# Gated messages of a graph network: gate operands in PSUM, five blocks a bank, rows added in seven operations, edge features loaded three batches ahead

## The chip, the core and the metric

The kernel runs on one core of a Trainium2 chip. Its engines are PE (TensorE, matmuls), DVE (VectorE), ACT (ScalarE), POOL (GpSimd, which here issues the indirect gathers) and SP (SyncE, which issues the plain transfers). The metric is the time of the whole program on the device, in microseconds (us), as the median of several runs. Lower is better.

## The reference, cut to what matters

Four graph layers follow one another on 6,250 nodes with 96 features and 200,000 edges sorted by destination. The change touches only the edge part of the third, the layer of gated messages:

```python
edge_input = concatenate([x[src], edge_attr], axis=-1)        # 96 + 32 features
messages = gelu(edge_input @ mW1 + mb1) @ mW2 + mb2
gates = sigmoid(gelu(edge_input @ gW1 + gb1) @ gW2 + gb2)     # one number per edge
aggregated = segment_sum(messages * gates, dst, num_segments=N)
```

## The kernel before, in words

The node parts `x @ mW1` and `x @ gW1` are computed once per node and stored in DRAM as `table_mg`, a row of 2 x 96 numbers per node (message half, gate half). The edges are padded and cut into 128 contiguous chunks, one per partition; a step takes one edge of every chunk, and `U` = 14 steps make a batch. There are `BATCHES` = 112 batches, 1,568 steps. The fast path of the stage is the function `sum_pass` of each engine; a batch n goes as follows.

- **SP** (L619 to L634) loads the batch's edge features, transposed, 256 KB, into one of two slots of `EA`, and waits until PE is done with the slot (`edge_product`, L622). In its loop, in order: the load for batch k+2, the wait for the running sums of batch k, the store of these sums to `run_m` (L633).
- **PE** (L1193 to L1200) multiplies them with block-diagonal weights `BD`: four edges stand in a group of 128 partitions, each edge giving 2 x 96 columns. A matmul gives two edges, 384 columns, in a bank of PSUM; `BANKS` = 7 products a batch. Eight banks `p_h` are used in turn, so PE runs ahead of ACT by eight products.
- **ACT** copies each product to `hid` in SBUF (`keep_edges`, L1574 to L1582), two batches ahead (`AHEAD_E`); there are four slots. For batch n it applies gelu to two halves (L1591), then tanh to the 14 logits per partition (L1593, `gates`; a sigmoid is written as half of 1 + tanh of the half), then copies the products of batch n+2.
- **POOL** (L824 to L828) issues 14 gathers per batch, one per step: 128 rows of `table_mg`, chosen by a column of indices `sources` in SBUF, into one of two slots of `rows`. The instruction stands at L790. Gathers of batch k wait for the additions of batch k-2 (`rows_added`, L826).
- **DVE** (L2229 to L2269) adds the gathered rows to `hid` in two operations of 1,344 elements per partition (L2235). It then makes the running sums of batch n-1, 14 dependent operations of 97 elements (L2263), and the messages of batch n: the gate half times the gate weights (L2243), the sum over features (L2246), then, after ACT's tanh, message half times (gate + 1) (L2248) and the gate's own column (L2250). The loop is `add_rows(n)`, `run_sums(n - 1)`, `messages(n)`.

So the order on each engine is written out by hand, and counts of semaphores couple them: `edge_product`, `edges_kept`, `rows_landed`, `rows_added`, `gelu_done`, `logit_ready`, `gate_ready`, `sums_ready`, `sums_stored`. The gate weights `gate_row` are a row repeated on all partitions in SBUF (`gw2`), and `gates` a part of the SBUF tile `small`. Before the stage, node matmuls (L1098, with DVE's L2136 emptying their banks) run beside the first two batches' gathers; behind it, the sums at each node's last edge are gathered from `run_m` (also L790) and the node part of the layer follows.

Of the kernel before, what the change touches and what calls it, by code (L numbers as in the profile page):

```python
# [11 lines left out]
ALU = mybir.AluOpType  # L12
ACT = mybir.ActivationFunctionType
# [4 lines left out]
D = 96  # L18
# [11 lines left out]
CH = P  # L30
U = 14
# [3 lines left out]
BATCHES = 2 * ITER  # L35
# [3 lines left out]
EG = 4  # L39
UG = -(-U // EG)  # L40
PIECES = 4
BANKS = 7
assert U == 2 * BANKS
ROOM = 16
AHEAD_E = 2
SLOTS_E = 4
MW = D + 1
AW = D + HEADS
ACCS = 3
# [88 lines left out]
def build(nc, x, src, dst, row_heads, src_rows, dst_rows, edge_t, consts, weights, bias, gcn_b, scalars, gate_w, mg_edge, qk_w, out):  # L138
# [21 lines left out]
    with ExitStack() as ctx:  # L160
# [24 lines left out]
        EA = sb("EA", [P, 2, UG, CH])  # L185
# [11 lines left out]
        small = sb("small", [CH, 4, U * HEADS])  # L197
# [5 lines left out]
        gw2 = sb("gw2", [P, D])  # L203
        sc = sb("sc", [P, 2])
        BD = sb("BD", [P, EG, 2, D])
# [132 lines left out]
        p_tr = [ps(f"p_tr{k}", [P, 512]) for k in (0, 1)]  # L338
        p_mm = [ps(f"p_mm{k}", [P, 512]) for k in (0, 1)]
        p_c = [*p_tr, *p_mm]  # L340
        p_four = ps("p_e", [P, 4, 512])
        p_e = [p_four[:, k, :] for k in range(4)]
        p_h = [*p_e, *p_tr, *p_mm]
        p_pair = p_four[:, 0:2, :]
        p_last = [p_e[HEADS - 1], p_tr[1]]
        p_sums = p_tr[0]
        gate_row = gw2[0:CH, :]
        gates = small[:, 1, 0:U]
        rows = GA[0:CH, 0:2 * U * 2 * D].rearrange("p (h u f) -> p h u f", h=2, u=U)
        hid_at = [*[GA[0:CH, (2 + k) * U * 2 * D:(3 + k) * U * 2 * D] for k in range(SLOTS_E - 1)], VA[0:CH, 0:U * 2 * D]]  # L350
        hid = [a.rearrange("p (u f) -> p u f", u=U) for a in hid_at]
# [116 lines left out]
        def wait(eng, s, v):  # L468

            if not isinstance(v, int) or v > 0:  # L470
                eng.wait_ge(s, v)
# [51 lines left out]
        def products(groups, n_w):  # L523

            return sum(len(bank_tiles(g, n_w)) for g in range(groups))

        def acc_steps(a):

            return len(range(a, U, ACCS))
# [38 lines left out]
        def _(sp):  # L568
# [49 lines left out]
            def sum_pass():  # L618

                def load_batch(k):  # L620
                    if k >= 2:
                        sp.wait_ge(edge_product, BANKS * (k - 1))  # L622
                    sp.dma_start(EA[:, k % 2, :, :], edge_t[:, UG * k:UG * (k + 1), :]).then_inc(edge_landed[k % 2], 16)
                load_batch(0)
                load_batch(1)
                sp.wait_ge(rows_cleared, 1)
                sp.dma_start(run_m[E:E + 2 * P, :].rearrange("(p k) f -> p k f", k=2), R[:, 1, 0:2, :]
                             ).then_inc(spares_stored, 16)
                for k in range(BATCHES):
                    if k + 2 < BATCHES:  # L630
                        load_batch(k + 2)
                    sp.wait_ge(sums_ready[k % 2], k // 2 + 1)
                    sp.dma_start(by_chunk(run_m[0:E, :])[:, U * k:U * (k + 1), :], R[:, k % 2, :, :]  # L633
                                 ).then_inc(sums_stored[k % 2], 16)  # L634
# [153 lines left out]
        def _(pool):  # L788
# [31 lines left out]
            def sum_pass():  # L820

                pool.wait_ge(sources_landed, 16)
                pool.wait_ge(table_stored, 16 * GROUPS * 2)
                for k in range(2 * ITER):  # L824

                    wait(pool, rows_added, 2 * (k - 1))  # L826
                    for j in range(U):
                        gather(rows[:, k % 2, j, :], table_mg, sources[:, U * k + j:U * k + j + 1], rows_landed[k % 2])  # L828

                pool.wait_ge(sums_ready[1], ITER)  # L830
                pool.indirect_dma_start(out=run_m, out_offset=bass.IndirectOffsetOnAxis(ap=open_at[:, 0:1], axis=0),
                                        in_=R[:, 1, U - 1, :], in_offset=None, compute_op=ALU.add).then_inc(open_added, 16)
                pool.wait_ge(nodes_landed, 32)
                for h in (0, 1):
                    pool.wait_ge(sums_stored[h], 16 * ITER)
                pool.wait_ge(open_added, 16)
                for t in range(TILES):
                    gather(AGG[:, t, :], run_m, ends[:, t:t + 1], ends_landed[t // GRP])
# [80 lines left out]
        def _(pe):  # L919
# [267 lines left out]
            def sum_pass():  # L1187


                pe.wait_ge(hT_ready, at["turn"])  # L1190
                pe.wait_ge(product_used, at["mm"])

                for m in range(BANKS * BATCHES):  # L1193
                    n, k = m // BANKS, m % BANKS
                    if k == 0:
                        pe.wait_ge(edge_landed[n % 2], 16 * (n // 2 + 1))
                    wait(pe, edges_kept, m - len(p_h) + 1)
                    pe.matmul(p_h[m % len(p_h)][0:CH, 0:4 * D], EA[:, n % 2, k // 2, :],  # L1198
                              BD[:, 2 * (k % 2):2 * (k % 2) + 2, :, :].rearrange("p a b f -> p (a b f)"),
                              start=True, stop=True).then_inc(edge_product, 1)  # L1200
                pe.wait_ge(edges_kept, BANKS * BATCHES)
                update_nodes()

            def scatter_pass(n):
# [176 lines left out]
        def _(act):  # L1381
# [190 lines left out]
            def sum_pass():  # L1572

                def keep_edges(n):  # L1574

                    wait(act, sums_ready[n % 2], (n - SLOTS_E) // 2 + 1)
                    for k in range(BANKS):
                        m = BANKS * n + k
                        act.wait_ge(edge_product, m + 1)
                        act.activation(hid[n % SLOTS_E][:, 2 * k:2 * k + 2, :],  # L1580
                                       p_h[m % len(p_h)][0:CH, 0:4 * D].rearrange("p (a f) -> p a f", a=2), ACT.Copy
                                       ).then_inc(edges_kept, 1)  # L1582

                act.wait_ge(table_stored, 16 * GROUPS * 2)
                for n in range(AHEAD_E):
                    keep_edges(n)
                for n in range(BATCHES):
                    for c in (0, 1):
                        half = hid[n % SLOTS_E][:, BANKS * c:BANKS * (c + 1), :]
                        act.wait_ge(rows_added, 2 * n + c + 1)  # L1590
                        act.activation(half, half, ACT.Gelu).then_inc(gelu_done, 1)  # L1591
                    act.wait_ge(logit_ready, n + 1)
                    act.activation(gates, small[:, 0, 0:U], ACT.Tanh, bias=half_bias, scale=0.5).then_inc(gate_ready, 1)  # L1593
                    if n + AHEAD_E < BATCHES:
                        keep_edges(n + AHEAD_E)
# [117 lines left out]
        def _(dve):  # L1713
# [510 lines left out]
            def sum_pass():  # L2224

                dve.tensor_scalar(half_bias, sc[0:CH, 1:2], 0.5, None, ALU.mult)
                dve.drain()

                def add_rows(n):  # L2229

                    dve.wait_ge(edges_kept, BANKS * (n + 1))
                    dve.wait_ge(rows_landed[n % 2], 16 * U * (n // 2 + 1))
                    for c in (0, 1):
                        half = hid[n % SLOTS_E][:, BANKS * c:BANKS * (c + 1), :]
                        dve.tensor_tensor(half, half, rows[:, n % 2, BANKS * c:BANKS * (c + 1), :], ALU.add  # L2235
                                          ).then_inc(rows_added, 1)

                def messages(n):

# [357 lines left out]
```

## Time and profile before

| what | value |
|---|---|
| median of 3 runs | 5472.3 us (5466.99 to 5479.78) |
| profiled execution, its own time | 5465.93 us |
| its span, first to last instruction | 5464.0 us |
| busy in the span: PE, DVE, ACT, POOL | 3652, 3789, 2527, 3537 us |
| gathers of `table_mg`, start of the first and of the last | 1519.8 and 3842.4 us of the span |

The page of the profile gives for each group of instructions its source line, engine, operation, tiles and shapes, the count behind an x, the busy time and mean duration, and the idle time of that engine just before with what ended it. "issue" is time in which an engine waited for nothing that the profile shows. SPq is the queue in which SP issues transfers. Times in a timeline are microseconds from the start of the span. POOL's rows are rougher than those of the other engines.

### The profile page before, as it was taken

What the parts mean: (1) busy time and instruction counts of PE and PEld (TensorE: products, weight loads), DVE (VectorE), ACT (ScalarE), POOL (GpSimd) and SP (SyncE); (2) the same over time, 40 slices, a digit from 0 to 9 for tenths busy, and PEclk for the clock granted to TensorE, in tenths of its full rate; (3) what the DMA queues carried; (4) which work ended last, traced back from release to release, by engine and by line L of the source; (5) the groups of instructions that cost most, each with busy time, mean ns of one, the idle gap of its engine ahead of it and who ended that gap; (6) DMA issues with size and microseconds to landing.
All of it is one profiled execution on the core that took longest, in us unless ns stands there. A gap on an engine that the chain in (4) does not pass through costs nothing.

```text
span 5464.0 us, 92238 instructions
## 1 busy us (share of the span) xinstructions
PE 3652.2 (67%) x33772; PEld 2286.6 (42%) x33772; DVE 3789.0 (69%) x5678; ACT 2527.0 (46%) x4379; POOL 3536.7 (65%) x2920
## 2 busy tenths in 40 slices
PE   4899899999953333333333333333279999999999
PEld 3888899899931111111111111111233333333333
DVE  7999432544455665665665655655379999999999
ACT  5999110101023233233333233332158888888887
POOL 3699100000057777777777777777448888888888
PEclk9999999999966666666666666666589999999999
DMA  3344889698733333333333333333111212222121
GB/s 70 165 200 191 331 340 394 256 398 336 292 90 115 117 114 115 118 110 117 117 110 119 117 111 117 117 111 118 46 35 57 64 57 60 60 58 64 57 63 38
DMA packets 296561, 760.10 MB, mean 139 GB/s; under 512 B 81161, under 2 KB 183753, under 8 KB 289993
## 3 DMA queue, kind: packets, MB, share of 16 engines
q1 hardware_dynamic: 217496, 595.47, 29.4%
q0 software_dynamic: 78768, 160.85, 11.2%
q8 instruction: 167, 2.74, 0.2%
q14 instruction: 130, 1.06, 0.1%
HBM read 589.77 MB, written 166.38 MB: 138 GB/s over the span
## 4 chain that ended last, share of the span: by engine, by line
PE 41%; POOL 34%; issue 15%; DVE 6%; ACT 1%; another core or an unknown queue 1%; DVEq 1%; DMA 0%; ACTq 0%; POOLq 0%; SPq 0%
POOL GA L790 32%; PE p_e L1167 14%; PE p_tr L1307 10%; PE p_e L1292 9%; PE p_mm L1269 3%; PE p_mm L1098 1%; POOL VA L790 1%; DVE VA L2423 1%; PE p_tr L1026 1%; DVE VA L1965 1%; POOL VA L902 1%; PE p_tr L1085 1%; DVE VA L1963 1%; PE p_e L1244 0%
## 5 line engine op out<-in xcount | busy, mean ns | idle before, releaser
L790 POOL DMA_INDIRECT GA<-table_mg,VA x1568 | 1791.1, 1142 | 1487.9 <-DMA table_mg<-VA 955.4
L2423 DVE TENSOR_TENSOR VA<-VA,p_mm 128x1024 f32<-128x1024 f32 (+1 forms) x1204 | 1362.0, 1203 | 7.5 <-POOL VA L902 6.6
L902 POOL TENSOR_SCALAR VA<-VA 128x1024 f32<-128x1024 f32 (+1 forms) x1204 | 1236.2, 1046 | 168.8 <-ACT VA L1644 157.0
L1198 PE MATMUL p_e<-BD,EA 128*128 128x384 f32 x784 | 407.1, 671 | 731.9 <-DMA EA<-in_edge_t 731.3
L1644 ACT ACTIVATE VA<-p_e 128x1024 f32<-128x1024 f32 x602 | 615.8, 1023 | 178.6 <-PE p_e L1292 177.5
L1307 PE MATMUL p_tr<-VA,GA 128*32 128x512 f32 (+1 forms) x5096 | 641.8, 580 | 2.7 <-ACT GA L1664 2.1
L2235 DVE TENSOR_TENSOR GA<-GA 128x1344 f32<-128x1344 f32 x168 | 254.2, 1554 | 542.7 <-DMA GA<-table_mg,VA 530.1
L2263 DVE SCALAR_TENSOR_TENSOR R<-R,keep,M 128x97 f32<-128x97 f32 x1568 | 505.8, 323 | 124.8 <-issue 8.2
L1198 PEld LDWEIGHTS p_e<-BD,EA 128*128 128x128 f32 x784 | 205.0, 270 | 916.9 <-DMA EA<-in_edge_t 765.1
L1198 PE MATMUL p_tr<-BD,EA 128*128 128x384 f32 x392 | 210.8, 669 | 370.9 <-DMA EA<-in_edge_t 370.9
L1198 PE MATMUL p_mm<-BD,EA 128*128 128x384 f32 x392 | 207.4, 660 | 374.0 <-DMA EA<-in_edge_t 374.0
L1292 PE MATMUL p_e<-T,GA 32*128 32x512 f16 x4632 | 444.9, 380 | 1.8 <-DVE GA L2392 1.1
L815 POOL TENSOR_TENSOR T<-T,B 128x192 f32 (+1 forms) x23 | 383.8, 16719 | 72.1 <-DVE T L1938 72.1
L1593 ACT ACTIVATE small<-small 128x14 f32<-128x14 f32 x112 | 34.4, 307 | 844.4 <-DVE small L2246 844.4
L1167 PE MATMUL p_e<-GA 128*128 128x192 f16 x4802 | 412.2, 246 | 0.0
L1167 PE MATMUL p_e<-GA,VA 128*128 128x192 f16 x4802 | 412.2, 246 | 0.0
L1167 PEld LDWEIGHTS p_e<-GA,VA 128*128 128x128 f16 x4802 | 397.7, 98 | 0.0
L1167 PEld LDWEIGHTS p_e<-GA 128*128 128x128 f16 x4802 | 397.6, 98 | 0.3 <-DVE M L2179 0.3
L1512 ACT ACTIVATE hT<-p_tr 96x512 f32<-96x512 f32 (+1 forms) x91 | 51.1, 567 | 717.3 <-PE p_tr L1085 689.3
L1646 ACT ACTIVATE VA<-p_e 128x512 f32<-128x512 f32 x602 | 356.3, 592 | 0.0
L2176 DVE SCALAR_TENSOR_TENSOR M<-p_e,dinv_s,T 128x96 f32<-128x96 f32 x196 | 62.3, 318 | 399.3 <-PE p_e L1167 399.1
L1198 PEld LDWEIGHTS p_tr<-BD,EA 128*128 128x128 f32 x392 | 102.8, 271 | 464.2 <-DMA EA<-in_edge_t 388.1
(267 smaller groups left out, 6616.6 us busy)
## 6 DMA issues: line engine op xcount, KB each, us to landing
GA<-adj SPq DMA_DIRECT2D x98, 800.0 KB, 6.1
VA<-adj SPq DMA_DIRECT2D x98, 800.0 KB, 6.1
run_m<-R SPq DMA_DIRECT2D x112, 700.0 KB, 3.9
GA<-adj SPq DMA_DIRECT2D x98, 768.0 KB, 6.1
VA<-adj SPq DMA_DIRECT2D x98, 768.0 KB, 6.1
H<-adj SPq DMA_DIRECT2D x56, 896.0 KB, 5.1
adj<-GA SPq DMA_DIRECT2D x25, 1568.0 KB, 5.3
adj<-VA SPq DMA_DIRECT2D x24, 1568.0 KB, 5.3
```

What stands on the lines that cost most here:

```text
L790: pool.indirect_dma_start(out=to, out_offset=None, in_=of, in_offset=bass.IndirectOffsetOnAxis(ap=at, axis=0)).then_inc(s, 16)
L815: pool.tensor_tensor(pair, pair, bias_row, ALU.add).then_inc(biased, 2)
L902: pool.tensor_scalar(e, e, HIGH, LOW, ALU.min, ALU.max).then_inc(clipped, 1)
L1167: mm = pe.matmul(p_e[b % 2][:, 0:PARTS * D], blk[b][:, s * P:(s + 1) * P], parts[:, s, :, :].rearrange("p k f -> p (k f)"), start=s == 0, ...
L1198: pe.matmul(p_h[m % len(p_h)][0:CH, 0:4 * D], EA[:, n % 2, k // 2, :], BD[:, 2 * (k % 2):2 * (k % 2) + 2, :, :].rearrange("p a b f -> p (a ...
L1292: mm = pe.matmul(to(e, cols), kT[rows, k // 2, d * P:(d + 1) * P], qT[b][rows, k % 2, 0:across(b)], start=k == 0, stop=k == 2, tile_positi ...
L1307: mm = pe.matmul(p_sums[e * HW:(e + 1) * HW, 0:across(b)], Vt[:, d, e, :], slot[n % SLOTS][:, e, i * across(b):(i + 1) * across(b)], start ...
L1644: act.activation(e[:, 0:2, :], p_pair[:, :, 0:cols], ACT.Exp, scale=HEADS_UNIT ** -2).then_inc(exps_ready, 1)
L1646: act.activation(e[:, 2, :], p_e[2][:, 0:cols], ACT.Exp, scale=HEADS_UNIT ** -2).then_inc(exps_ready, 1)
L2235: dve.tensor_tensor(half, half, rows[:, n % 2, BANKS * c:BANKS * (c + 1), :], ALU.add).then_inc(rows_added, 1)
L2263: op = dve.scalar_tensor_tensor(out=R[:, h, j, 0:MW], in0=before, scalar=keep[:, step:step + 1], in1=M[:, j, 0:MW], op0=ALU.mult, op1=ALU.add)
L2423: dve.tensor_tensor(e, e, p_mm[n % 2][:, 0:cols_of(n)].unsqueeze(1).to_broadcast([P, 2, cols_of(n)]), ALU.mult).then_inc(weighed, 1)
```

## The change

Constants: products are packed by `PACK` = 5 blocks of 96 columns, so a batch's 28 blocks take `PACKS` = 6 banks (480 columns, the last 288). `ADDS` = 7 additions a batch. PE's packs cross the groups of four edges, so a pack is one or two matmuls: nine products of one to five blocks for a batch. PSUM's last bank is taken out of the rotation (seven are left) and holds the gate weights, copied there once, and the gates. ACT's gelu is cut 8 steps and 6 steps. SP loads three batches before the loop and keeps that lead; there are still two slots of `EA`.

```diff
+PACK = 5
+PACKS = -(-2 * U // PACK)
+ADDS = BANKS
@@ build
-        p_h = [*p_e, *p_tr, *p_mm]
+        p_h = [*p_e, *p_tr, p_mm[0]]
-        gate_row = gw2[0:CH, :]
-        gates = small[:, 1, 0:U]
+        gate_row = p_mm[1][0:CH, 0:D]
+        gates = p_mm[1][0:CH, D:D + U]
+        def pack_halves(b):
+            return range(PACK * b, min(PACK * b + PACK, 2 * U))
+        def pack_cols(b):
+            return slice(D * pack_halves(b).start, D * pack_halves(b).stop)
@@ SP
-                        sp.wait_ge(edge_product, BANKS * (k - 1))
+                        sp.wait_ge(edge_product, PACKS * (k - 1))
-                load_batch(0)
-                load_batch(1)
+                for k in range(AHEAD_E + 1):
+                    load_batch(k)
...
-                    if k + 2 < BATCHES:
-                        load_batch(k + 2)
+                    if k + AHEAD_E + 1 < BATCHES:
+                        load_batch(k + AHEAD_E + 1)
@@ POOL
-                    wait(pool, rows_added, 2 * (k - 1))
+                    wait(pool, rows_added, ADDS * (k - 1))
@@ PE
-                for m in range(BANKS * BATCHES):
-                    n, k = m // BANKS, m % BANKS
-                    if k == 0:
+                for m in range(PACKS * BATCHES):
+                    n, b = m // PACKS, m % PACKS
+                    if b == 0:
                         pe.wait_ge(edge_landed[n % 2], 16 * (n // 2 + 1))
                     wait(pe, edges_kept, m - len(p_h) + 1)
-                    pe.matmul(p_h[m % len(p_h)][0:CH, 0:4 * D], EA[:, n % 2, k // 2, :],
-                              BD[:, 2 * (k % 2):2 * (k % 2) + 2, :, :].rearrange("p a b f -> p (a b f)"),
-                              start=True, stop=True).then_inc(edge_product, 1)
+                    at_col = 0
+                    for g in range(UG):
+                        part = [v for v in pack_halves(b) if v // (2 * EG) == g]
+                        if not part:
+                            continue
+                        cols = slice(D * (part[0] - 2 * EG * g), D * (part[-1] + 1 - 2 * EG * g))
+                        mm = pe.matmul(p_h[m % len(p_h)][0:CH, at_col:at_col + D * len(part)], EA[:, n % 2, g, :],
+                                       BD[:, :, :, :].rearrange("p a b f -> p (a b f)")[:, cols], start=True, stop=True)
+                        at_col += D * len(part)
+                    mm.then_inc(edge_product, 1)
@@ ACT
-                    for k in range(BANKS):
-                        m = BANKS * n + k
+                    for b in range(PACKS):
+                        m = PACKS * n + b
                         act.wait_ge(edge_product, m + 1)
-                        act.activation(hid[n % SLOTS_E][:, 2 * k:2 * k + 2, :],
-                                       p_h[m % len(p_h)][0:CH, 0:4 * D].rearrange("p (a f) -> p a f", a=2), ACT.Copy
-                                       ).then_inc(edges_kept, 1)
+                        act.activation(hid_at[n % SLOTS_E][:, pack_cols(b)], p_h[m % len(p_h)][0:CH, 0:D * len(pack_halves(b))],
+                                       ACT.Copy).then_inc(edges_kept, 1)
...
-                    for c in (0, 1):
-                        half = hid[n % SLOTS_E][:, BANKS * c:BANKS * (c + 1), :]
-                        act.wait_ge(rows_added, 2 * n + c + 1)
-                        act.activation(half, half, ACT.Gelu).then_inc(gelu_done, 1)
+                    for lo, hi in ((0, BANKS // 2 + 1), (BANKS // 2 + 1, BANKS)):
+                        some = hid[n % SLOTS_E][:, 2 * lo:2 * hi, :]
+                        act.wait_ge(rows_added, BANKS * n + hi)
+                        act.activation(some, some, ACT.Gelu).then_inc(gelu_done, 1)
@@ DVE
                 dve.tensor_scalar(half_bias, sc[0:CH, 1:2], 0.5, None, ALU.mult)
+                dve.tensor_copy(gate_row, gw2[0:CH, :])
                 dve.drain()
...
-                    dve.wait_ge(edges_kept, BANKS * (n + 1))
+                    dve.wait_ge(edges_kept, PACKS * (n + 1))
                     dve.wait_ge(rows_landed[n % 2], 16 * U * (n // 2 + 1))
-                    for c in (0, 1):
-                        half = hid[n % SLOTS_E][:, BANKS * c:BANKS * (c + 1), :]
-                        dve.tensor_tensor(half, half, rows[:, n % 2, BANKS * c:BANKS * (c + 1), :], ALU.add
-                                          ).then_inc(rows_added, 1)
+                    for k in range(BANKS):
+                        two = hid[n % SLOTS_E][:, 2 * k:2 * k + 2, :]
+                        dve.tensor_tensor(two, two, rows[:, n % 2, 2 * k:2 * k + 2, :], ALU.add).then_inc(rows_added, 1)
```

## Rows read from the trace of the kernel before

**Rows 1.** Busy time per engine from 1600 to 3800 us, inside the stage

```profile
core 0: us, PE busy (x) PEld busy (x) DVE busy (x) ACT busy (x) POOL busy (x), PEclk, DMA share, GB/s
1600.00:3800.00 2200.00, 752.02 (x1502) 394.79 (x1503) 1320.64 (x2144) 684.07 (x1072) 1717.77 (x1500) 0.67 0.38 115
```

**Rows 2.** Chain of waits from 1600 to 3800 us, by line

```profile
by line: POOL GA L790 78.1%; issue 21.9%
```

**Rows 3.** POOL's groups from 1600 to 3800 us: count, busy, mean ns, idle before

```profile
L790 POOL DMA_INDIRECT GA<-table_mg,VA x1500 | 1718.1, 1145 | 482.5 <-issue 482.5
```

**Rows 4.** Timeline of POOL, gathers 1, 28 and 29: start, duration, idle before

```profile
1519.82 0.97 POOL L790 DMA_INDIRECT GA<-table_mg,VA  x1 [955.42 <-DMA table_mg<-VA]
...
1553.67 0.95 POOL L790 DMA_INDIRECT GA<-table_mg,VA  x1 [0.30 <-issue]
1584.47 0.95 POOL L790 DMA_INDIRECT GA<-table_mg,VA  x1 [29.84 <-DVE GA L2235]
```

**Rows 5.** Timeline of one batch, DVE's operations and the gathers over them

```profile
2510.05 3.02 DVE L2235 TENSOR_TENSOR GA<-GA 128x1344 f32<-128x1344 f32 x2 [6.24 <-DMA GA<-table_mg,VA]
2511.11 1.33 POOL L790 DMA_INDIRECT GA<-table_mg,VA  x1 [0.30 <-issue]
...
2512.74 1.16 POOL L790 DMA_INDIRECT GA<-table_mg,VA  x1 [0.30 <-issue]
2513.17 5.48 DVE L2263 SCALAR_TENSOR_TENSOR R<-R,keep,M 128x97 f32<-128x97 f32 x14
...
2518.74 1.56 DVE L2243 TENSOR_TENSOR M<-GA,gw 128x1344 f32<-128x1344 f32 x1
...
2519.21 1.90 POOL L790 DMA_INDIRECT GA<-table_mg,VA  x1 [0.30 <-issue]
2520.37 1.55 DVE L2246 TENSOR_REDUCE small<-M 128x14 f32<-128x1344 f32 x1
2521.42 0.94 POOL L790 DMA_INDIRECT GA<-table_mg,VA  x1 [0.30 <-issue]
...
2522.30 1.56 DVE L2248 SCALAR_TENSOR_TENSOR M<-small,GA 128x1344 f32<-128x1344 f32 x1 [0.37 <-ACT small L1593]
2522.67 2.01 POOL L790 DMA_INDIRECT GA<-table_mg,VA  x1 [0.30 <-issue]
```

**Rows 6.** Timeline: a batch's last gather, the next adds, a late gather

```profile
2527.49 0.95 POOL L790 DMA_INDIRECT GA<-table_mg,VA  x1 [0.30 <-issue]
...
2530.22 3.03 DVE L2235 TENSOR_TENSOR VA<-VA,GA 128x1344 f32<-128x1344 f32 x2 [6.28 <-DMA GA<-table_mg,VA]
...
2531.94 2.13 POOL L790 DMA_INDIRECT GA<-table_mg,VA  x1 [2.25 <-issue]
```

**Rows 7.** Attention, later: POOL's L902 and DVE's L2423, ns min/median/max, first and last start

```profile
L902 POOL TENSOR_SCALAR VA<-VA x1204: 827/1042/1365, 4058.4 to 5453.0; 128x1024 f32<-128x1024 f32 x170, 128x768 f32<-128x768 f32 x2
...
L2423 DVE TENSOR_TENSOR VA<-VA,p_mm x1204: 894/1206/1222, 4059.6 to 5454.5; 128x1024 f32<-128x1024 f32 x170, 128x768 f32<-128x768 f32 x2
```

**Rows 8.** DVE lines over the whole span, ns min/median/max, first and last start

```profile
L2263 DVE SCALAR_TENSOR_TENSOR R<-R,keep,M x1568: 320/321/389, 1593.8 to 3864.3; 128x97 f32<-128x97 f32 x196
...
L2235 DVE TENSOR_TENSOR GA<-GA x168: 1548/1553/1560, 1581.2 to 3826.4; 128x1344 f32<-128x1344 f32 x168
...
L2136 DVE TENSOR_TENSOR T<-p_mm,B x38: 247/350/559, 1488.7 to 1570.4; 128x192 f32<-128x192 f32 x24, 128x384 f32<-128x384 f32 x12, 128x96 f32<-128x96 f32 x2
```

**Rows 9.** Timeline of one batch: edge load, tanh, PE's products, ACT's first and last copy

```profile
2519.05 0.43 SPq L623 DMA_DIRECT2D EA<-in_edge_t  x1
...
2521.96 0.31 ACT L1593 ACTIVATE small<-small 128x14 f32<-128x14 f32 x1 [7.52 <-DVE small L2246]
...
2523.24 4.67 PE L1198 MATMUL p_e<-BD,EA 128*128 128x384 f32 x8 [13.49 <-DMA EA<-in_edge_t]
...
2524.99 0.49 ACT L1580 ACTIVATE GA<-p_e 128x384 f32<-128x384 f32 x1 [2.72 <-PE p_e L1198]
...
2529.88 0.49 ACT L1580 ACTIVATE GA<-p_mm 128x384 f32<-128x384 f32 x1 [0.15 <-PE p_mm L1198]
```

More of the change, by code:

```diff
@@ L1191, in sum_pass @@
                 pe.wait_ge(product_used, at["mm"])
-                for m in range(BANKS * BATCHES):
-                    n, k = m // BANKS, m % BANKS
-                    if k == 0:
+                for m in range(PACKS * BATCHES):
+                    n, b = m // PACKS, m % PACKS
+                    if b == 0:
                         pe.wait_ge(edge_landed[n % 2], 16 * (n // 2 + 1))
                     wait(pe, edges_kept, m - len(p_h) + 1)
-                    pe.matmul(p_h[m % len(p_h)][0:CH, 0:4 * D], EA[:, n % 2, k // 2, :],
-                              BD[:, 2 * (k % 2):2 * (k % 2) + 2, :, :].rearrange("p a b f -> p (a b f)"),
-                              start=True, stop=True).then_inc(edge_product, 1)
-                pe.wait_ge(edges_kept, BANKS * BATCHES)
+                    at_col = 0
[8 more added lines that the diff above has]
+                    mm.then_inc(edge_product, 1)
+                pe.wait_ge(edges_kept, PACKS * BATCHES)
                 update_nodes()
```

## The prediction

> **What bounds the kernel now.** I read the stage first: the gated messages run from 1,520 to 3,865 us, and in the 2,200 us from 1,600 to 3,800 no engine is full: POOL is busy for 1,718 us, DVE for 1,321, PE for 752, ACT for 684, DMA for 0.38 of the time [rows 1]. So a busy share doesn't settle it. The chain of waits of the same stretch does: 78.1% POOL's gathers (L790), 21.9% "issue", which is the pause between one gather and the next, and nothing else [rows 2]. POOL is the bound, gather after gather, and its share is under 100% only because the 0.30 us pauses are not counted as busy.
>
> The pace: 1,500 gathers in 2,200 us are 1.467 us each [rows 3], and a batch of 14 takes 20.53 us. The same gathers alone, while DVE has hardly begun, start (1553.67 - 1519.82) / 27 = 1.254 us apart [rows 4]; a batch would take 17.55 us. So 2.98 us a batch are stalls of POOL, over 110 batches (of 1,568 gathers 28 are issued before the first add; 1,540 / 14 = 110) 328 us. That is all that there is to win here.
>
> Where the stalls lie: in one batch gathers of 0.94 to 0.95 us stand beside one of 1.90, which ends 0.81 us after the product with the gate weights (L2243), and one of 2.01, which ends 0.82 us after the gating (L2248). The gather begun during the reduction (L2246) takes 0.94, those of 1.33 and 1.16 end 0.84 and 0.82 us after the first and the second add (L2235), and those over the 14 running sums (L2263) show nothing [rows 5]. So a gather needs, about 0.13 us after its start, something that a long DVE operation with two SBUF operands holds, and gets it when that operation ends. Per batch: L2243 0.95, L2248 1.06, together 2.01; what is left of 2.98, 0.97, goes to the two adds: mostly 0.38 + 0.21 = 0.59, and in some batches more, where the next gather starts 1.95 us late and then takes 2.13 [rows 6].
>
> **The change, part by part.**
> (a) Gate weights and gates in PSUM. L2243 and L2248 keep one SBUF input each. No row shows a gather over such a long operation; the nearest is in the attention: POOL's L902, 1,024 elements read from and written to SBUF, has a median of 1,042 ns, beside DVE's L2423, which reads SBUF and PSUM, writes SBUF and is at work all the time [rows 7]. Were it held off as gathers are here, it couldn't keep that pace. The reduction, one SBUF input, stalls nothing either. Bounds: 0 to 2.01 us a batch gained; I take 2.01, the nearer rows. The two DVE operations cost what they did: 384 elements with one PSUM operand take 559 ns at most and 1,024 take 1,206 [rows 7, 8], so 1,344 come to 559 + 960 x 1.011 = 1,530 ns against 1,559. Unseen is the gates' repeated read of one PSUM word; from the nearest rows it costs nothing, and DVE has room for 3.7 us (below). The one copy of the weights is some 0.2 us in all.
> The Trainium skill, "SBUF — State Buffer", section "Who interferes with whom", says that a DVE instruction with two SBUF inputs contends with GpSimd reads and one with at most one doesn't, but infers that a tensor_tensor takes only the read side and leaves descriptor generation, which writes, alone. The trace disagrees with that inference: the 1.90 us gather. If writes are what matters, moving an input gains nothing: that is rival B, priced from rows.
>
> (b) Seven adds for two. Each 384 elements: the first 0.56 us, the next at 1.47 - 960 x 1.04 ns = 0.47 us intervals (1.47 us is what the second 1,344-element add puts on top of 1.55, and (1553 - 559) / 960 = 1.04 ns an element) [rows 5, 8]: 3.40 us against 3.03. A gather waits for the end of one such add, not of 1.5 us. The adds start 2.73 us after the last gather of their batch [rows 6]; undisturbed gathers ask at 2.64 and 3.89 us after it, the second 1.16 us into the adds, in the third of them, and waits 0.3; the next asks 1.25 us later, near the end of the sixth, and waits 0.1 to 0.2. So 0.4 us a batch against 0.97. Bounds: nothing, as over the running sums of 321 ns, which have pauses between them; and 2.2 us, if back to back adds let nobody in until the last ends (3.4 - 1.2). I take 0.4, because between the two adds of now a gather does get in: it ended 0.84 us after the first, in the middle of the second [rows 5]. Gain 0.57.
>
> (c) Five blocks a bank. ACT's copies (L1580) change from seven of 0.49 us to, scaled by their columns, five of 0.61 and one of 0.37 [rows 9], PE's matmuls from 14 (two for a product) to 18 for the same 2,688 columns; PE at 34% has room [rows 1]. Neither is on the chain. PE has seven banks instead of eight, more than one batch of six.
>
> (d) Edge features three ahead. Now the load for batch k+2 is issued at 2519.05, PE starts on it at 2523.24, ACT, idle since its tanh ended at 2522.27, gets a product at 2524.99 and ends its copies at 2530.37 [rows 9], 20.3 us after the adds began, as the next adds begin. With the load a batch earlier the products wait in their banks, and ACT is done 12.6 + 4.2 = 16.8 us after the adds begin (tanh's end now 12.2, the adds 0.4 longer; copies 3.4 and five pauses of 0.15); its gelu is due about 19.9 (a batch of 17.95 and four adds). This pays nothing now, since the 5.5 us of running sums between adds and L2243 hide ACT's delay, but it keeps ACT clear of the shorter batch. SP's wait for PE's batch k+1 stands ahead of the store of sums k: PE finishes that batch once ACT has copied batch k, over a batch before SP asks. At the start the third load stands ahead of the spare rows' store, which DVE wants only two batches on. I cost (c) and (d) at nothing.
>
> **Who is next.** DVE's chain in a batch, from the adds to the end of L2248, is 2523.86 - 2510.05 = 13.8 us [rows 5], then 14.2; POOL's batch becomes 17.55 + 0.4 = 17.95, so DVE still idles 3.7 us for the last row and POOL stays the bound. The rows' slots: gathers of batch n+2 need the adds of n, finished some 14 us before.
>
> **The sum.** 110 x (2.01 + 0.57) = 284 us gained; about 1 us lost at the two ends (three more tenths of adds before the first and after the last gather, the copy). The profiled execution took 5465.9 us, so 5183; it stands 6.4 us under the median of the three runs, 5472.3, for which I say 5189.
>
> **Rivals.**
> A, the forecast: chance 0.80.
> B, PSUM doesn't free POOL: what holds it is DVE's stream of 1,344 elements written to SBUF, which L2243 and L2248 keep. For it: all three stalling operations write 1,344, the reduction 14. Against it: L902 beside L2423, which writes as much. Gain 110 x 0.57 = 63: 5409. Chance 0.08.
> C, the seven adds hold as one: 2.2 us a batch stay: 110 x (2.98 - 2.2) = 86 gained: 5386. For it the back to back adds, against it the gather let in between two. Chance 0.07.
> D, slower: the writes hold POOL as in B, and the adds are one unbroken stream of them. Then 2.01 stays and 2.2 replaces 0.97: 110 x 1.23 = 135 us more: 5607. It decides from the point where the adds cost over 0.97 us a batch with the other two unchanged. Against it both rows above at once. Chance 0.03.
> E, DVE becomes the bound because the broadcast read of PSUM is slow. From L2248 at 1.56 + 3.7 = 5.3 us on it takes gain away, from 7.8 us on (3.9 ns an element more than any row shows) the kernel is slower. Chance 0.02, mostly still faster.
>
> **Range and chances.** In A the adds' stall may lie between 0 (5145) and about 1.1 us (5266). 5145 to 5270 holds nearly all of A and so about 8 in 10; B and C lie above and are left out. About 0.2% (11 us) is what a measurement of this kernel can tell from no change. Faster 0.95 (A, B, C, part of E), same 0.01, slower 0.04.
>
> **What would show it.** Right: gathers over L2243 and L2248 of 0.95 us, none of 1.9 to 2.3; mean gather near 0.98 (1,145 ns now); L2235 seven times a batch, 3.4 us together; L2243 and L2248 within 0.1 us of 1.56; 14 gathers in about 18 us; the wait for edge features gone from ACT's copies; the chain still POOL's. Wrong: gathers of 1.9 us that end with L2243 or L2248 (B), one long gather ending 0.8 us after the seventh add (C), DVE's wait for the rows gone and its busy time in the chain (E).

## The result and the profile after

The changed kernel takes 5493.96 us in the median of 8 runs (5472.83 to 5512.74), against 5474.88 us for the kernel before in 8 runs (5466.99 to 5480.59). The ratio is 1.0038, with a 95% interval of 1.002 to 1.0057: 19 us slower, where 284 us of gain were forecast. The profiled execution took 5492.26 us with a span of 5490.5.

What the forecast rests on is in the profile all the same. DVE's two long operations over the PSUM operands, and the gathers beside them, in the timeline of the changed kernel (L2259 was L2243, L2264 was L2248, L800 was L790; compare [rows 5]):

```profile
2507.73 0.95 POOL L800 DMA_INDIRECT GA<-table_mg,VA  x1 [0.30 <-issue]
...
2508.98 0.95 POOL L800 DMA_INDIRECT GA<-table_mg,VA  x1 [0.30 <-issue]
2509.07 1.55 DVE L2259 TENSOR_TENSOR M<-GA,p_mm 128x1344 f32<-128x1344 f32 x1 [1.05 <-issue]
2510.24 0.95 POOL L800 DMA_INDIRECT GA<-table_mg,VA  x1 [0.30 <-issue]
...
2513.06 1.56 DVE L2264 SCALAR_TENSOR_TENSOR M<-p_mm,GA 128x1344 f32<-128x1344 f32 x1 [0.34 <-issue]
...
2514.62 3.36 DVE L2252 TENSOR_TENSOR GA<-GA 128x384 f32<-128x384 f32 x7
...
2515.25 1.20 POOL L800 DMA_INDIRECT GA<-table_mg,VA  x1 [0.30 <-issue]
...
2516.76 1.10 POOL L800 DMA_INDIRECT GA<-table_mg,VA  x1 [0.30 <-issue]
```

No gather is stretched by L2259 or L2264, and only two by the adds, by 0.25 and 0.15 us: 0.40 us a batch, as forecast. The seven adds take 3.36 us (forecast 3.40). The next view is of 1600 to 3800 us again: busy times per engine, the group of the gathers, and the chain of waits by line, to set beside [rows 1, 2, 3]:

```profile
1600.00:3800.00 2200.00, 801.83 (x1930) 459.18 (x1929) 1346.87 (x2672) 589.81 (x960) 1459.20 (x1504) 0.66 0.39 115
```

```profile
L800 POOL DMA_INDIRECT GA<-table_mg,VA x1504 | 1460.1, 971 | 771.4 <-issue 458.1 <-DVE GA L2252 208.6 <-remote 65.7
```

```profile
by line: DVEq L2274 22.2%; issue 19.5%; DVE R L2279 19.3%; DVE GA L2252 10.3%; DVE small L2262 6.6%; DVE M L2259 6.6%; another core or an unknown queue 5.3%; DVE VA L2252 3.5%; DVEq L2257 1.6%; ACT GA L1607 1.4%; ACT GA L1597 1.1%; ACT p_mm
```

The gathers fell from 1,145 to 971 ns in the mean, yet 1,504 of them pass in the 2,200 us, as good as the 1,500 of before. POOL now waits for DVE's adds (L2252, 209 us; nothing before), and the chain, POOL's alone before, is DVE's: its running sums (L2279) and the drains between them (L2274). The waits of the same stretch, longest first in total, with their number and the longest:

```profile
DVE R L2279 <- issue: 659.3, 544, 7.0
...
ACT GA L1597 <- remote: 265.7, 44, 10.7
...
POOL GA L800 <- DVE GA L2252: 208.6, 21, 32.8
```

In one such batch the running sums, 0.4 us apart before, stand 1.4 and 0.7 us apart, while the gathers beside them keep their pace. The first two rows are PE's products that the last three, ACT's copies, take:

```profile
2494.11 1.03 PE L1214 MATMUL p_mm<-BD,EA 128*128 128x96 f32 x4
2494.98 1.52 PE L1214 MATMUL p_e<-BD,EA 128*128 128x384 f32 x6
...
2501.26 0.32 DVE L2279 SCALAR_TENSOR_TENSOR R<-R,keep,M 128x97 f32<-128x97 f32 x1 [1.08 <-issue]
...
2502.66 0.34 DVE L2279 SCALAR_TENSOR_TENSOR R<-R,keep,M 128x97 f32<-128x97 f32 x1 [1.08 <-issue]
...
2503.40 0.32 DVE L2279 SCALAR_TENSOR_TENSOR R<-R,keep,M 128x97 f32<-128x97 f32 x1 [0.40 <-issue]
...
2521.05 0.57 ACT L1597 ACTIVATE GA<-p_mm 128x480 f32<-128x480 f32 x1 [6.61 <-remote]
...
2528.82 0.57 ACT L1597 ACTIVATE GA<-p_e 128x480 f32<-128x480 f32 x1 [7.19 <-remote]
...
2534.40 0.41 ACT L1597 ACTIVATE GA<-p_e 128x288 f32<-128x288 f32 x1 [5.02 <-remote]
```

The last three rows are the other half. ACT waits 5 to 7 us for each product ("remote" is another core or an unknown queue, and the kernel has one core), though PE had ended these three by 2495.1 and 2496.5, 26 to 38 us before they are copied; the signal is what comes late. I call this **the hold-up**: the increments of semaphores by PE and DVE, and the drains of DVE, are late, while POOL's gathers run on.

Three counts over the stage show its size. Product by product (the m-th copy of ACT against the m-th product of PE), 96 of the 672 copies start, after a wait, over 5 us after their product had ended, 48 us at most; in the kernel before none is over 0.4 us. By the records of semaphores, of the 565 recorded increments of `edge_product` (672 were made), 321 came more than 0.2 us after the product that had ended last, and 167 more than 5 us after it; in the kernel before, none of 671 recorded (784 made). This second count is a lower bound, since an increment can belong to an earlier product. And in 50 of the 112 batches the 14 running sums take over 6 us from the start of the first to that of the last, up to 19, against 5.2 in most batches of before (5.6 at most); together some 470 us more. A batch takes 18.2 us in the median and up to 33.8, 20.58 in the mean, against 20.54 before (the first two batches left out).

Of the 26.5 us between the two spans only 5 lie in the gathers' stage itself (first to last gather 2,327 against 2,323 us) and 8 behind it (36.6 against 28.3 us from the last gather to the first of the node sums, in which the last running sums are held up). Some 15 lie before the first gather (1534.6 against 1519.8 us), in code that the change leaves alone; the same changed kernel took 1524.1 us for that stretch in run f1 below, and the others 1512 to 1533, so most of the difference between the two spans says nothing of the stage.

### The profile page after: what moved, and what is told of

It reads as the page before. It is cut to its first block, busy times and chain, and to the rows that moved or that the text cites. A ratio compares the mean times of both kernels' runs of the same rounds, so it can differ in the third digit from the quotient of the medians.

```text
span 5490.5 us, 93583 instructions
## 1 busy us (share of the span) xinstructions
PE 3710.4 (68%) x34220; PEld 2358.0 (43%) x34220; DVE 3822.8 (70%) x6239; ACT 2432.5 (44%) x4267; POOL 3266.2 (59%) x2920
## 4 chain that ended last, share of the span: by engine, by line
PE 41%; DVE 25%; issue 14%; DVEq 11%; ACT 3%; another core or an unknown queue 3%; POOL 2%; DMA 0%; ACTq 0%; POOLq 0%; SPq 0%
PE p_e L1177 14%; PE p_tr L1324 10%; PE p_e L1309 9%; DVEq L2274 9%; DVE R L2279 8%; DVE GA L2252 4%; PE p_mm L1286 3%; DVE small L2262 3%; DVE M L2259 3%; DVE VA L2252 1%; PE p_mm L1108 1%; POOL VA L800 1%; DVE VA L2439 1%; PE p_tr L1036 1%
## 5 line engine op out<-in xcount | busy, mean ns | idle before, releaser
L800 POOL DMA_INDIRECT GA<-table_mg,VA x1568 | 1521.4, 970 | 1775.5 <-DMA table_mg<-VA 968.8
L1214 PE MATMUL p_e<-BD,EA 128*128 128x288 f32 (+4 forms) x1152 | 489.3, 582 | 822.0 <-DMA EA<-in_edge_t 568.2
L2279 DVE SCALAR_TENSOR_TENSOR R<-R,keep,M 128x97 f32<-128x97 f32 x1568 | 511.2, 326 | 751.2 <-issue 674.7
L1214 PEld LDWEIGHTS p_e<-BD,EA 128*128 128x128 f32 x1152 | 274.1, 265 | 1023.3 <-DMA EA<-in_edge_t 595.9
L1214 PE MATMUL p_tr<-BD,EA 128*128 128x384 f32 (+4 forms) x576 | 253.5, 585 | 399.2 <-DMA EA<-in_edge_t 275.3
L1609 ACT ACTIVATE p_mm<-small 128x14 f32<-128x14 f32 x112 | 30.9, 276 | 1100.9 <-DVE small L2262 552.1
L1214 PEld LDWEIGHTS p_tr<-BD,EA 128*128 128x128 f32 x576 | 137.8, 266 | 503.1 <-DMA EA<-in_edge_t 287.9
L2252 DVE TENSOR_TENSOR GA<-GA 128x384 f32<-128x384 f32 x588 | 282.7, 551 | 8.6 <-DMA GA<-table_mg,VA 8.4
L1059 PE MATMUL p_e<-VA 128*128 128x98 f16 x2352 | 263.3, 208 | 14.0 <-DVE VA L1981 13.8
```

The lines of the kernel that those rows point to most:

```text
L800: pool.indirect_dma_start(out=to, out_offset=None, in_=of, in_offset=bass.IndirectOffsetOnAxis(ap=at, axis=0)).then_inc(s, 16)
L1214: mm = pe.matmul(p_h[m % len(p_h)][0:CH, at_col:at_col + D * len(part)], EA[:, n % 2, g, :], BD[:, :, :, :].rearrange("p a b f -> p (a b f ...
L2252: dve.tensor_tensor(two, two, rows[:, n % 2, 2 * k:2 * k + 2, :], ALU.add).then_inc(rows_added, 1)
L2279: op = dve.scalar_tensor_tensor(out=R[:, h, j, 0:MW], in0=before, scalar=keep[:, step:step + 1], in1=M[:, j, 0:MW], op0=ALU.mult, op1=ALU.add)
```

## The experiments

The theories (lettered apart from the prediction's rivals): **A**, an unbroken stream of gathers holds up the signals of PE and DVE and DVE's drains, and the stalls that the change removes were the breaks in the stream. **B**, the seven increments of the adds flood the signals. **C**, the packs or the earlier load do it. Ratios are to the kernel before on the same chip, with their 95% intervals.

**e1, gate operands back in SBUF** (seven adds, packs and lead stay):

```diff
-        gate_row = p_mm[1][0:CH, 0:D]
-        gates = p_mm[1][0:CH, D:D + U]
+        gate_row = gw2[0:CH, :]
+        gates = small[:, 1, 0:U]
-                dve.tensor_copy(gate_row, gw2[0:CH, :])
```

> The changed kernel with gate weights and gates back in SBUF; seven adds, packs and the load ahead stay. Theory A (an unbroken stream of POOL's gathers holds up the semaphore signals of PE and DVE and DVE's drains; the stalls of POOL over DVE's long two-operand operations were the breaks in it): gathers of 1.9 to 2.0 us return over the two long DVE operations, the 14 running sums take 5.2 us in nearly every batch, a batch takes 20.0 us, time 5400 to 5430. Theory B (the seven semaphore increments of the adds flood the signals): running sums still take up to 18 us in many batches, time 5480 or more. Theory C (packs or the earlier load do it): the same, 5480 or more.

5404.38 us, ratio 0.9876 (0.9852 to 0.990). The timeline of e1 shows the stalls back (its L2258 and L2263 are the two long operations):

```profile
2515.53 1.56 DVE L2258 TENSOR_TENSOR M<-VA,gw 128x1344 f32<-128x1344 f32 x1
2516.01 1.91 POOL L800 DMA_INDIRECT GA<-table_mg,VA  x1 [0.30 <-issue]
...
2519.09 1.56 DVE L2263 SCALAR_TENSOR_TENSOR M<-small,VA 128x1344 f32<-128x1344 f32 x1 [0.38 <-ACT small L1609]
2519.47 2.01 POOL L800 DMA_INDIRECT GA<-table_mg,VA  x1 [0.30 <-issue]
```

and the running sums are over 6 us in 4 batches instead of 50, and 9 copies are over 5 us late instead of 96. Taking the forecast's larger gain out makes the kernel 90 us faster. The adds, packs and lead are worth 68 us; B and C fall as the main cause.

**e2, the kernel before with the PSUM operands alone**; **e3, the changed kernel with two adds.**

```diff
e2, on the kernel before
-        p_h = [*p_e, *p_tr, *p_mm]
+        p_h = [*p_e, *p_tr, p_mm[0]]
-        gate_row = gw2[0:CH, :]
-        gates = small[:, 1, 0:U]
+        gate_row = p_mm[1][0:CH, 0:D]
+        gates = p_mm[1][0:CH, D:D + U]
+                dve.tensor_copy(gate_row, gw2[0:CH, :])
e3, on the changed kernel
-ADDS = BANKS
+ADDS = 2
...
+                    for c in (0, 1):
+                        half = hid[n % SLOTS_E][:, BANKS * c:BANKS * (c + 1), :]
+                        dve.tensor_tensor(half, half, rows[:, n % 2, BANKS * c:BANKS * (c + 1), :], ALU.add
+                                          ).then_inc(rows_added, 1)
```

> The kernel before with gate weights and gates in PSUM (seven product banks), nothing else. Theory A: POOL's only breaks are the two adds, so part of the batches show running sums of over 10 us and signals of PE that come over 5 us late; a batch takes 19 to 21 us, time 5400 to 5500. Theories B and C: no held up signals, a batch takes 18.5 us (17.55 + 0.97), time about 5250.

> The changed kernel with two adds again (and gelu in halves). Theory A: like e2, 5400 to 5500, with held up signals. Theory B: running sums of 5.2 us throughout, time about 5250. Theory C: as the changed kernel, about 5494.

e2: 5491.96 us, 1.0022 (0.9996 to 1.0048); e3: 5501.26 us, 1.0042 (1.0027 to 1.0056). Both show the hold-up: PE's recorded increments over 5 us late are 102 of 603 in e2 and 78 of 561 in e3, running sums over 6 us 12 and 39. PSUM alone brings it on; the number of increments is not needed for it. e2 leaves the two adds' stalls (0.97 us a batch by the prediction's estimate), and they are not break enough.

**e4, four blocks a bank and edge features two ahead**, the changed kernel with `PACK = 4` and the two loads and `load_batch(k + 2)` of before.

> The changed kernel with four blocks a bank (seven products a batch) and edge features loaded two ahead. Theories A and B: as the changed kernel, 5475 to 5515, running sums of up to 18 us. Theory C: running sums of 5.2 us throughout, a batch of 18 us, time about 5190.

5621.51 us, 1.0275 (1.024 to 1.031): outside what A expected, though not on C's side. In e4 PE waits 1,389 us for edge features in the stage, and ACT 616 us for late signals in 156 waits. With the hold-up, one more product a batch whose signal is late, and a load issued a batch later, cost 128 us together (which of the two costs what, no run tells); so my "nothing" for these two parts holds only where signals come in time (e12).

**e5 to e8, breaks that have nothing to do with DVE.** The changed kernel, with POOL clearing unused elements between gathers:

```diff
                         gather(rows[:, k % 2, j, :], table_mg, sources[:, U * k + j:U * k + j + 1], rows_landed[k % 2])
+                        if j % 7 == 6:
+                            count = (U // 7) * k + j // 7
+                            wait(pool, gathered_used[1], count)
+                            pool.memset(GA[:, 14000:14000 + 1024], 0.0).then_inc(gathered_used[1], 1)
```

(e6: 128 elements; e7: every 14, 1,024; e8: every 2, 128. The semaphore only orders one clearing behind the last.)

> The changed kernel, with POOL clearing 1,024 unused elements per partition after every seventh gather: a break of about 1 us in the stream of gathers, twice a batch, that has nothing to do with DVE or PSUM. Theory A (the unbroken stream holds up the signals of PE and DVE): with streaks of seven gathers the signals come in time, the running sums take 5.2 us in all but a few batches, a batch takes 17.55 + 0.4 + 2 x 1.0 to 2 x 1.2 = 20.0 to 20.4 us, time 5405 to 5455, less spread from batch to batch. Rival (something else in the change, PSUM above all, holds up the signals, and POOL merely runs beside it): the running sums still take up to 18 us and the time is above 5500, since POOL has less time to catch up.

> The same with 128 elements, a break of 0.2 to 0.4 us. If the mere interruption is enough, signals come in time and a batch takes 18.4 to 18.8 us, time 5230 to 5280. If it is the mean pace of the gathers that counts, or the break has to be as long as POOL's stalls (about 1 us), the signals are still held up in part of the batches, time 5400 to 5500.

> One break of about 1 us after every fourteenth gather. Theory A with a stream of over about ten gathers as the condition: held up signals at the end of the streak, fewer than in the changed kernel, a batch 19 to 21 us, time 5300 to 5500. If one break a batch is enough: a batch of 19.0 us, time about 5300.

> A break of 0.2 to 0.4 us after every second gather, seven a batch, so the mean pace falls like in e5 but without a long break. If the mean pace counts: signals in time, a batch of 19.4 to 20.7 us, time 5370 to 5490, like e5. If a break has to be long: held up signals remain and the time is above 5450.

e5: 5379.58 us, 0.9827 (0.981 to 0.9843), 114 us faster than the changed kernel though POOL does 1.6 us more in each batch. No copy of ACT starts, after a wait, over 0.4 us after its product had ended, and none of PE's recorded increments (496 of 672) is over 0.2 us late; the running sums are 5.4 us in the median and never over 6, and the batches take 19.5 to 20.6 us. The chain of waits in e5 from 1600 to 3700 us is POOL's again (L842 is the clearing), and the running sums stand close:

```profile
by line: POOL GA L800 69.3%; issue 20.9%; POOL GA L842 9.8%
```

```profile
2502.16 5.47 DVE L2283 SCALAR_TENSOR_TENSOR R<-R,keep,M 128x97 f32<-128x97 f32 x14
```

This is what settles theory A on that chip: PSUM, adds, packs and lead are all as in the changed kernel, and only POOL's stream differs. The same trace has the counterpart. Behind the stage the 49 gathers of the node sums (3787.9 to 3847.9 us) have no breaks, and some 16 us after they begin ACT's waits for PE are long again:

```profile
3822.68 0.60 ACT L1560 ACTIVATE hT<-p_tr 97x512 f32<-97x512 f32 x1 [17.87 <-issue]
3833.88 0.59 ACT L1560 ACTIVATE hT<-p_tr 96x512 f32<-96x512 f32 x1 [10.60 <-issue]
```

The breaks don't cure everything: beside the first 28 gathers ACT and DVE still wait up to 7.2 and 6.5 us, where f5 below, on a chip without the hold-up, has 3.4 and 2.7. e5 was somewhat faster than expected (5405 to 5455), as a break put 0.82 us between gathers and not 1.0 to 1.2.

e6: 5450.16 us, 0.9958 (0.9939 to 0.9976). e7: 5472.36 us, 1.0005 (0.9981 to 1.003). e8: 5480.18 us, 1.0014 (0.9989 to 1.0039). All three keep the hold-up, with running sums over 6 us in 44, 39 and 52 batches. Their batches take 18.1, 18.8 and 18.5 us in the median: 1.29, 1.34 and 1.32 us a gather. e5's gathers are 1.40 us apart, e1's 1.39 with the hold-up all but gone, those of before 1.44 and more. A clearing of 128 elements takes 0.22 us but puts only 0.08 us between two gathers, not the 0.2 to 0.4 expected: e6 had hardly a break, and e8 didn't reach e5's mean pace, which it was made to test.

**e9 to e12** went to another chip, where the kernel before took 5412.84 us, not 5474.

> A break after every second gather, with 320 elements: about 0.38 us of clearing, 0.25 us added each time, seven times a batch. The mean pace of the gathers then is that of e5, 1.40 us, but no break is long. If the pace counts: signals in time, a batch of 19.5 to 19.8 us with little spread, time 5370 to 5390. If the length of a break counts: the running sums still take up to 18 us in many batches, time 5430 or more.

> A break after every seventh gather, with 512 elements: about 0.54 us, 0.4 us added, a batch of 18.7 us and a pace of 1.335 us if nothing is held up. If the pace counts, with its threshold near 1.40: held up signals remain, as in e7 (1.33), time 5420 to 5480. If streaks of seven with a break of any length over 0.3 us are enough: time 5270 to 5300.

> e5 with the same breaks in the 49 gathers of the node sums behind the stage as well (six breaks, 5 us). In the kernel before, ACT waits 19 us twice for a signal of PE beside these gathers. If breaks let such signals through here too, the node part ends sooner after the last gather, and the time is 0 to 20 us under e5's 5380; otherwise about 5 us over it.

> e4 (four blocks a bank, edge features two ahead) with e5's breaks. Theory A: packs and lead cost or gain nothing once the signals come in time, so 5375 to 5395, as e5; that e4 was 128 us slower than the changed kernel would be due to its seventh signal of PE and later loads while signals were held up. If packs and lead matter by themselves: over 5400.

e9: 5363.31 us, 0.9916 (0.9895 to 0.9937). e10: 5249.53 us, 0.9703 (0.9686 to 0.9719). e11: 5327.82 us, 0.9846 (0.9829 to 0.9863). e12: 5332.22 us, 0.9853 (0.9836 to 0.9871). None has a late increment or a late copy, and none has the held-up waits beside the node sums' gathers (2.6 us at most, behind a first wait of 21 that f5 has too), where e9, e10 and e12 have no breaks either. So these four couldn't tell pace from length of a break, nor what breaks bring to the node sums: there was nothing to cure. e12 against e11 does say that packs and lead are worth nothing measurable in the stage once signals are in time: from first to last gather it lasts 2218.0 and 2218.3 us. The two ratios' intervals overlap. The question became whether the hold-up is there on every chip.

**f1 to f4**, the same kernels once more:

> The changed kernel itself, beside the kernel before on the same chip. Theory A1 (the hold-up of signals beside an unbroken stream of gathers is there on some chips and not on others): where ACT waits 19 us beside the 49 gathers of the node sums, as on the chip of e1 to e8, the time is 1.002 to 1.006 of the kernel before; where those waits are 3 us at most, as on the chip of e9 to e12, a batch takes 17.9 to 18.3 us and the ratio is 0.945 to 0.955. Theory A2 (the hold-up is everywhere, and e9 to e12 escaped it by their breaks alone): 1.00 to 1.01 on any chip.

> The kernel before, with a profile on this chip. A batch of 20.2 to 20.6 us with gathers of 1.9 and 2.0 us over DVE's two long operations, on any chip. Beside the first 28 and the last 49 gathers ACT waits 19 us for PE's signal where the hold-up exists, and under 8 and under 4 us where it doesn't; then the time is near 5410 rather than 5475.

> e10 again. On a chip with the hold-up: if the pace of the gathers counts with its threshold near 1.40 us, held up signals remain and the ratio to the kernel before is 0.99 to 1.00; if streaks of seven with a break of 0.4 us are enough, 0.965 to 0.970. On a chip without it the breaks only cost: 0.970 again, 90 us over the changed kernel.

> e2 again: the kernel before with the gate operands in PSUM alone. On a chip without the hold-up PSUM's own share shows: 2.0 us a batch, a ratio of 0.955 to 0.962. On one with it: 1.00 as before.

They came to a third chip, one with the hold-up. f1, the changed kernel: 5493.15 us, 1.0032 (1.001 to 1.0054). f2, the kernel before: 5474.74 us in one run; ACT's longest waits beside the first 28 and the last 49 gathers are 17 and 24 us, where 19 were forecast. f3, e10's kernel: 5477.29 us, 1.0002 (0.9986 to 1.0018), running sums over 6 us in 38 batches. f4, PSUM alone: 5527.13 us, 1.0104 (1.0072 to 1.0136), clear of e2's 0.9996 to 1.0048: the size of the loss isn't the same on every chip that has the hold-up. f3 and e5 differ in the length of the break, 512 against 1,024 elements at streaks of seven, and so in pace, 1.34 against 1.40 us, and in the chip: on this one, streaks of seven with 0.4 us between them are not enough.

**f5, the changed kernel a third time; f6, PSUM alone a third time:**

> The changed kernel once more, beside the kernel before. Where the waits of ACT beside the node sums' gathers are 3 us at most and the kernel before takes about 5413: theory A1 has a batch of 17.9 to 18.3 us, running sums of 5.2 us throughout and a ratio of 0.945 to 0.955; theory A2 has held up signals and 1.00 there too. Where those waits are 19 us, both have 1.002 to 1.006.

> e2 a third time: gate operands in PSUM alone. Where the kernel before takes about 5413 and the changed one 0.953 of that: two adds and gathers stalled by them alone, a batch of 18.5 to 18.7 us, ratio 0.958 to 0.964. Where the kernel before takes about 5474: held up signals, 1.00 to 1.01.

f5 came to a chip without the hold-up: **5158.08 us against 5414.57, ratio 0.953 (0.9514 to 0.9546)**. The chain of waits from 1600 to 3500 us, the gathers' group there, and the busy times:

```profile
by line: POOL GA L800 75.3%; issue 24.8%
```

```profile
L800 POOL DMA_INDIRECT GA<-table_mg,VA x1461 | 1430.4, 979 | 471.1 <-issue 471.1
```

```profile
1600.00:3500.00 1900.00, 755.66 (x1890) 445.48 (x1888) 1319.68 (x2606) 570.30 (x939) 1429.16 (x1461) 0.69 0.43 130
```

A batch takes 18.0 us in the median, 18.21 in the mean; the running sums are never over 6 us, no increment and no copy is late, and every increment of the whole trace is on record. That is so on e9 to e12's chip too, while each trace from the chips with the hold-up lacks some: 428 of 13,270 in the kernel before, 496 of 13,830 in e5, 1,112 of 13,606 in the changed kernel. The timeline shows the adds as they were forecast, DVE idle for 3 us before them:

```profile
2512.36 3.37 DVE L2252 TENSOR_TENSOR GA<-GA 128x384 f32<-128x384 f32 x7 [2.99 <-DMA GA<-table_mg,VA]
...
2513.42 1.26 POOL L800 DMA_INDIRECT GA<-table_mg,VA  x1 [0.30 <-issue]
...
2514.98 1.11 POOL L800 DMA_INDIRECT GA<-table_mg,VA  x1 [0.30 <-issue]
```

f6 met the hold-up on yet another chip: 5546.09 us, 1.0118 (1.0091 to 1.0144), a little over the 1.00 to 1.01 expected. What PSUM alone gains where signals come in time stays unmeasured.

In seven groups of runs (the official result, e1 to e4, e5 to e8, e9 to e12, f1 to f4, f5, f6), the last six on five different chips, the kernel before took 5471 to 5476 us in five, each with the hold-up, and 5413 and 5415 in two, without any. Half of these 60 us stands behind the last of the node sums' 49 gathers: from there to the end it is 1533 and 1535 us in the kernel before and f2, and 1502 to 1503 in e9 to e12 and f5, whichever edge stage stood ahead.

## Why the prediction was wrong

**What held.** POOL bounds the kernel before, by stalls of 2.98 us a batch. PSUM operands free POOL from L2243 and L2248 entirely (2.01 us; gathers over them take 0.95 us), by the rows of all runs with them: rival B, and with it the inference cited from the Trainium skill, "SBUF — State Buffer", section "Who interferes with whom", is out as far as it would spare gathers from a tensor_tensor with two SBUF operands, and that section's other rule, that one SBUF input doesn't contend, is borne out. The seven adds cost 0.40 us in the rows of the changed kernel and 0.47 in those of f5 (1.26 + 1.11 - 2 x 0.95), against 0.4: rival C is out. They last 3.37 us, against 3.40; L2259 and L2264 take 1,554 and 1,558 ns, so rival E is out. Where signals come in time the whole sum holds: 256 us gained against 284. The rest of 28 is the mean batch of 18.2 us against 17.95.

**What failed** is the step "Who is next", in its last clause that POOL stays the bound, and the sentence that costed (c) and (d) at nothing. Both took for granted that the other engines work beside a faster POOL as they did beside a slow one. On the chip of the official result they don't: their signals and drains are late when gathers follow one another at 1.25 us for long, and the stalls that the change removes were what kept the mean pace at 1.47. The loss isn't a new term of some size, it is the whole gain: the median batch falls from 20.2 to 18.2 us, and the batches of 20 to 34 us, four in ten, give it back, so that the mean stays at 20.6 where 17.95 was forecast.

**It was there to be read.** The kernel before has two stretches in which gathers meet no long DVE operation: the first 28, from 1520 to 1555 us, and the 49 of the node sums. In its trace the waits of the first one, from 1519 to 1560 us (two rows), and of the second, from 3870 to 3935, are:

```profile
ACT hT L1512 <- remote: 27.9, 3, 19.1
DVE T L2136 <- remote: 24.2, 2, 14.9
...
ACT hT L1539 <- remote: 29.8, 2, 19.2
```

A wait of 19 us for a matmul that takes one, twice, both times beside gathers 1.254 us apart. I took [rows 4] from that very stretch as the pace "alone", and looked at POOL only. In f5 the first stretch (1500 to 1560 us) has no wait for "remote" at all; ACT's longest wait for PE is 3.4 us:

```profile
ACT hT L1529 <- PE p_tr L1095: 28.5, 19, 3.4
```

**Rival D** had the sign right and the mechanism wrong: no gather is held by writes.

## What stays open

Which resource gathers and signals share isn't shown, nor why some chips have the hold-up. That records of semaphores are missing on just the chips that have it, in every kernel, e5 included, may mean that recording takes part in it; all runs here were recorded, so no run excludes it. The late copies themselves don't rest on those records: ACT's waits and PE's products are rows of their own. Whether the mean pace decides (held up at 1.29 to 1.34 us a gather, free at 1.40) or the length of a break along with its distance (free with 0.82 us every seven, held up with 0.4 every seven and 0.8 every fourteen) isn't told apart: e9 was made for that and came to a chip without the hold-up.

## What to carry to other kernels

A stall can be a brake that others live by: before removing one, look for a stretch of the same trace where it is absent already, and read what all engines, not only the freed one, do there. A wait for "remote" or "issue" of many microseconds beside work that has ended is a row to be explained, not skipped. Where the hold-up exists, a small break on POOL, 0.8 us every seven gathers, turned +0.4% into -1.7% (e5) and beat both kernels; where it doesn't, breaks only cost (ratios 0.970 to 0.992 with them, 0.953 without, on two such chips; 0.985 for e5's break, e11), so the choice depends on which chips the kernel will meet.

## What was unexpected of the hardware

- Beside gathers 1.25 us apart a quarter of DVE's drains between the running sums last 1.3 us or more instead of 0.33, and signals of PE arrive over 5 us late, up to 48 us after their product; the gathers themselves aren't slower (0.95 us).
- On the chips with the hold-up part of the semaphores' records is missing in every trace, on the others in none.
- The same two kernels stand at a ratio of 1.003 on one chip and 0.953 on another, and the kernel before itself differs by 60 us (5474 against 5413).
- With the hold-up, one product a batch more and loads a batch later cost 128 us (e4); without it, nothing measurable (e12).
